# Moving three elementwise steps of the feed-forward part from VectorE to ScalarE in a Mamba-plus-ternary-FFN kernel

## The chip, the cores and the metric

The kernel runs as one program on all 8 cores of one Trainium2 chip. Each core works on its own 2048 tokens; there is no traffic between the cores apart from their common memory. The metric is the device time in microseconds (us) of the slowest core, and the profile is of that core (core 7 here). The engines are PE (TensorE), DVE (VectorE), ACT (ScalarE), POOL (GpSimd) and SP (SyncE), each with its own instruction queue that it works through in order.

## The reference

For 16384 tokens of 1024 numbers, the output is `x + mamba(layernorm(x)) + ffn(layernorm(x))`. Only the feed-forward part is touched by the change:

```python
def _act_quant(x):
    scale = 127.0 / clip(max(abs(x), axis=-1), 1e-05)
    return clip(round(x * scale), -128.0, 127.0) / scale
def _weight_quant(w):
    scale = 1.0 / clip(mean(abs(w)), 1e-05)
    return clip(round(w * scale), -1.0, 1.0) / scale
bitlinear = lambda x, w: einsum('bsi,oi->bso', _act_quant(x), _weight_quant(w))
ffn = lambda x: bitlinear(silu(bitlinear(x, w_gate)) * bitlinear(x, w_up), w_down)
```

The hidden width is 4096. Quantised activations are integers up to 127 and quantised weights are -1, 0 or 1; both are held in bf16, and the scales are multiplied in when a result leaves PSUM.

## The kernel before, in words

A small recording layer (`P.op`) takes each instruction with the names of what it reads and writes, puts it at the end of its engine's queue, and adds the waits on semaphores that those names ask for. The order in each queue is therefore the order in which the Python code calls `P.op`; generators that yield one instruction at a time are interleaved by hand. A buffer that is written again waits for its last reader.

The program has four stages on each core: layer norm and the casting of weights; the Mamba part with its scans (most of the time); F1, the gate and up projections with silu; and F2, the down projection and the final sum. A barrier over all queues stands between the stages. The change is in F1 and F2.

**F1** runs over 8 column blocks f of 512 columns. For each f, `f1_mm(f)` runs over 16 token tiles mt of 128 tokens. A tile is 8 matmuls into a gate bank, 8 into an up bank, and then four steps: gsb (L918, ACT, silu of the gate bank times a per-token scale), usb (L921, DVE, the up bank times a per-token scale), gu_bf (L924, DVE, the product of the two) and gmparts (L928, DVE, its largest magnitude). There are three gate banks (psB, psG2, psG3) and three up banks (psC, psU2, psU3), used in turn, and two buffers each of gsb and usb. So the first up matmul of tile mt+3 waits for usb of tile mt, and gsb of tile mt waits for gu_bf of tile mt-2.

Beside the tiles of block f, a second stream `_sec(f)` does two other jobs. It quantises the gate and up weights for block f+1: a load from HBM on SP into one of two buffers wqf, then L891 and L895 on DVE, sixteen times. And in blocks 0 to 5 it quantises the down weights: a load into the single buffer wqf3, then L957 and L960 on DVE into the single buffer wdstg, and a store on POOL (L965) to the HBM tensor s_wdq. `_zipf` takes two steps of the tiles, then one of the second stream, so the second stream lies beside tiles 0 to 7 of a block, and tiles 8 to 15 have the engines to themselves. This document calls these the first and the second half of a block.

**F2** runs over 8 groups g of two token tiles. `f2_a(g)` requantises the hidden activations in four pieces per tile: tqg (L1041, DVE, scale and add the rounding bias 384.5), a mask (L1047, DVE), minus 384 (L1050, DVE, back into gu_bf); then 8 transposes per piece on PE (L1058) into the one bank psT, and ACT copies them out to guqT (L1065). `f2_b(g)` does the down matmuls (L1089) for both tiles, psB for the first and psC for the second, over two halves of 512 output columns. It loads 1 MB of s_wdq for every 16 matmuls into one of two buffers wdqt, ends each half with two scalings dnsb (L1100, DVE), and each group with four adds (L1108, L1112, DVE) and a store. `f2_a(g+1)` is interleaved with `f2_b(g)`, two steps to three, so one tile's requantising lies beside each half; `f2_a(0)` stands alone at the start of F2. There are two buffers tqg; the mask works in place.

Of the kernel before, what the change touches and what calls it, by code (L numbers as in the profile page):

```python
# [11 lines left out]
AF = mybir.ActivationFunctionType  # L12
ALU = mybir.AluOpType
# [12 lines left out]
RBIAS = 384.5  # L26
# [116 lines left out]
def build_program(TOK):  # L143
# [29 lines left out]
    P = Prog(nc)  # L173
# [4 lines left out]
    def salloc(stack, name, shape, dt):  # L178
        return stack.enter_context(nc.sbuf_tensor(name, shape, dt))
# [8 lines left out]
    combou = salloc(pstack, "combou", [128, NT], F32)  # L188
    combod = salloc(pstack, "combod", [128, NT], F32)
    gmparts = salloc(pstack, "gmparts", [128, NT * 8], F32)  # L190
    sgu = salloc(pstack, "sgu", [128, NT], F32)
    invsgu = salloc(pstack, "invsgu", [128, NT], F32)
    ones1 = salloc(pstack, "ones1", [128, 1], F32)
    csts = salloc(pstack, "csts", [128, 3], F32)
# [607 lines left out]
    for sc in range(NSC):  # L802
# [7 lines left out]
        else:  # L810
# [12 lines left out]
                            for t2 in range(32)],  # L823
         writes=["psA"], wr_override=["psA"])
    P.op("scalar", lambda s: s.activation(acc[0:1, 0:96], psA[0:1, 0:96], AF.Copy,
                                          bias=0.0, scale=1.0),
# [31 lines left out]
    usb = [salloc(fstk, "usb%d" % i, [128, 512], BF16) for i in range(2)]  # L858
# [42 lines left out]
    def f1_mm(f):  # L901
        fb = f % 2
        for mt in range(NT):
            gb = mt % 2
            psg, psgt = psGpool[mt % 3]
            psu, psut = psUpool[mt % 3]
            for (wtag, ps_, pst_) in (("wgq", psg, psgt), ("wuq", psu, psut)):
                wq_ = wgq[fb] if wtag == "wgq" else wuq[fb]
                for k2 in range(8):
                    yield lambda wq_=wq_, k2=k2, mt=mt, ps_=ps_, pst_=pst_, wtag=wtag, fb=fb: P.op(  # L910
                        "tensor", lambda t: t.matmul(  # L911
                            ps_[:, 0:512],
                            xqfm[:, k2 * TOK + mt * 128:k2 * TOK + (mt + 1) * 128],
                            wq_[:, k2 * 512:(k2 + 1) * 512], start=(k2 == 0), stop=(k2 == 7)),
                        reads=["xqfm:%d" % k2, "%s:%d:%d" % (wtag, fb, k2)],
                        writes=([pst_] if k2 == 0 else ()),
                        wr_override=([pst_] if k2 == 7 else ()))
            yield lambda gb=gb, mt=mt, psg=psg, psgt=psgt: P.op("scalar", lambda s: s.activation(  # L918
                gsb[gb][:], psg[:, 0:512], AF.Silu, bias=0.0, scale=combog[:, mt:mt + 1]),
                reads=[psgt, "cg:%d" % mt], writes=["gsb:%d" % gb])  # L920
            yield lambda gb=gb, mt=mt, psu=psu, psut=psut: P.op("vector", lambda v: v.tensor_single_scalar(  # L921
                usb[gb][:], psu[:, 0:512], combou[:, mt:mt + 1], ALU.mult),
                reads=[psut, "cu:%d" % mt], writes=["usb:%d" % gb])
            yield lambda gb=gb, mt=mt, f=f: P.op("vector", lambda v: v.tensor_mul(  # L924
                gu_bf[:, mt * INNER + f * 512:mt * INNER + (f + 1) * 512],
                gsb[gb][:], usb[gb][:]),
                reads=["gsb:%d" % gb, "usb:%d" % gb], writes=["gu:%d:%d" % (mt, f)])
            yield lambda gb=gb, mt=mt, f=f: P.op("vector", lambda v: v.reduce_max(  # L928
                gmparts[:, mt * 8 + f:mt * 8 + f + 1],
                gu_bf[:, mt * INNER + f * 512:mt * INNER + (f + 1) * 512],  # L930
                axis=AXX, apply_absolute_value=True),
                reads=["gu:%d:%d" % (mt, f)], writes=["gmp:%d:%d" % (mt, f)])
# [62 lines left out]
    for f in range(8):  # L995
        _zipf(iter(f1_mm(f)), _sec(f), 2, 1)
# [33 lines left out]
    dnsb = [salloc(f2stk, "dnsb%d" % i, [128, DM], F32) for i in range(2)]  # L1030
# [4 lines left out]
    def f2_a(g):  # L1035
        gb = g % 2
        mts = (2 * g, 2 * g + 1)
        for j, mt in enumerate(mts):
            for hh in range(4):
                hb = hh % 2  # L1040
                yield lambda mt=mt, hh=hh, hb=hb: P.op("vector", lambda v: v.tensor_scalar(  # L1041
                    tqg[hb][:], gu_bf[:, mt * INNER + hh * 1024:mt * INNER + (hh + 1) * 1024],
                    sgu[:, mt:mt + 1], RBIAS, ALU.mult, ALU.add),
                    reads=["gu:%d:%d" % (mt, f2) for f2 in range(hh * 2, hh * 2 + 2)]
                          + ["sgu:%d" % mt],
                    writes=["tqg:%d" % hb])
                yield lambda hb=hb: P.op("vector", lambda v: v.tensor_single_scalar(  # L1047
                    tmg[hb][:].bitcast(I32), tqg[hb][:].bitcast(I32), RMASK, ALU.bitwise_and),
                    reads=["tqg:%d" % hb], writes=["tqg:%d" % hb])
                yield lambda mt=mt, hh=hh, hb=hb: P.op("vector", lambda v: v.tensor_single_scalar(  # L1050
                    gu_bf[:, mt * INNER + hh * 1024:mt * INNER + (hh + 1) * 1024],
                    tmg[hb][:], -384.0, ALU.add),
                    reads=["tqg:%d" % hb] + ["gu:%d:%d" % (mt, f2) for f2 in range(hh * 2, hh * 2 + 2)],
                    writes=["guqq:%d:%d" % (mt, hh)])
            for gb8 in range(4):
                for kb in range(8):
                    kk = gb8 * 8 + kb
                    yield lambda mt=mt, kk=kk, kb=kb: P.op("tensor", lambda t: t.matmul(  # L1058
                        psT[:, kb * 128:(kb + 1) * 128],
                        gu_bf[:, mt * INNER + kk * 128:mt * INNER + (kk + 1) * 128],  # L1060
                        eye[:], is_transpose=True, start=(kb == 0), stop=(kb == 7)),
                        reads=["guqq:%d:%d" % (mt, kk // 8), "eye"],
                        writes=(["psT"] if kb == 0 else ()),
                        wr_override=(["psT"] if kb == 7 else ()))
                yield lambda j=j, gb8=gb8, gb=gb: P.op("scalar", lambda s: s.activation(  # L1065
                    guqT[gb][j][:, gb8 * 1024:(gb8 + 1) * 1024], psT[:, 0:1024], AF.Copy,
                    bias=0.0, scale=1.0),
                    reads=["psT"], writes=["guqT:%d:%d:%d" % (gb, j, gb8)])

    def f2_b(g):  # L1070
        gb = g % 2
        mts = (2 * g, 2 * g + 1)
        for f2 in range(2):
            for kc in range(4):
                wb3 = kc % 2
                yield lambda kc=kc, f2=f2, wb3=wb3: P.op("sync", lambda e: e.dma_start(
                    wdqt[wb3][:].rearrange("part (k c) -> part k c", k=8),
                    s_wdq.ap()[kc * 1024:(kc + 1) * 1024,
                               f2 * 512:(f2 + 1) * 512].rearrange(
                        "(k part) c -> part k c", k=8)),  # L1080
                    reads=["swdq:%d:%d" % (kc * 8 + k3, f2) for k3 in range(8)],
                    writes=["wdqt:%d" % wb3], dma=True)
                for k3 in range(8):
                    kb = kc * 8 + k3
                    for j, mt in enumerate(mts):
                        ps_ = psB if j == 0 else psC
                        pst_ = "psB" if j == 0 else "psC"
                        yield lambda j=j, kb=kb, k3=k3, wb3=wb3, ps_=ps_, pst_=pst_, gb=gb: P.op(
                            "tensor", lambda t: t.matmul(  # L1089
                                ps_[:, 0:512], guqT[gb][j][:, kb * 128:(kb + 1) * 128],  # L1090
                                wdqt[wb3][:, k3 * 512:(k3 + 1) * 512],
                                start=(kb == 0), stop=(kb == 31)),
                            reads=["guqT:%d:%d:%d" % (gb, j, kb // 8), "wdqt:%d" % wb3],
                            writes=([pst_] if kb == 0 else ()),
                            wr_override=([pst_] if kb == 31 else ()))
            for j, mt in enumerate(mts):
                ps_ = psB if j == 0 else psC
                pst_ = "psB" if j == 0 else "psC"
                yield lambda j=j, mt=mt, f2=f2, ps_=ps_, pst_=pst_: P.op(
                    "vector", lambda v: v.tensor_single_scalar(  # L1100
                        dnsb[j][:, f2 * 512:(f2 + 1) * 512], ps_[:, 0:512],
                        combod[:, mt:mt + 1], ALU.mult),
                    reads=[pst_, "cd:%d" % mt], writes=["dn:%d:%d" % (j, f2)])
        for j, mt in enumerate(mts):
            yield lambda j=j, mt=mt: P.op("sync", lambda e: e.dma_start(
# [14 lines left out]
    for fn in f2_a(0):  # L1120
        fn()
    for g in range(NT // 2):
        nxt = iter(f2_a(g + 1)) if g + 1 < NT // 2 else iter(())
        _zipf(iter(f2_b(g)), nxt, 3, 2)
# [82 lines left out]
```

How the kernel before makes its waits and increments, by code:

```python
                def body(eng, lst=lst, q=q):  # L119
                    sat = {}
                    last_inc = {}
                    for o in lst:
                        wl = {}
                        for d in o.waits:
                            if d.cum > wl.get(d.skey, 0):
                                wl[d.skey] = d.cum
                        for k in sorted(wl, key=lambda t: (t[0], t[1])):
                            v = wl[k]
                            if v > sat.get(k, 0):
                                eng.wait_ge(sems[k], v)
                                sat[k] = v
                        inst = o.fn(eng) if o.fn is not None else None
                        if o.inc:
                            k = o.skey
                            amt = o.cum - last_inc.get(k, 0)
                            inst.then_inc(sems[k], amt)
                            last_inc[k] = o.cum
```

## Time and profile before

| what | value |
|---|---|
| median of 2 timed runs | 5410.28 us (5409.01 to 5411.56) |
| the profiled execution's own time | 5414.21 us |
| its span (core 7, first to last instruction) | 5412.6 us; 5371.2 to 5412.6 us over the cores |
| DVE busy over the span | 4078.4 us (75%) |
| ACT busy over the span | 1691.7 us (31%) |
| PE busy over the span | 1658.3 us (31%) |
| F1's blocks, by the trace | 4335 to 4963 us of the span |
| F2, by the trace | 4984 to 5413 us of the span |

The busy shares are averages over stages with different limits, so what the change is worth has to be read inside F1 and F2. A row of the timeline gives an instruction's start, its length, its engine, its line, and in square brackets how long its engine sat idle before it and what ended the idle time. The chain of waits follows the last instruction of a stretch back to what released it, step by step.

### The profile page before, as it was taken

What the parts mean: (1) busy time and instruction counts of PE and PEld (TensorE: products, weight loads), DVE (VectorE), ACT (ScalarE), POOL (GpSimd) and SP (SyncE); (2) the same over time, 40 slices, a digit from 0 to 9 for tenths busy, and PEclk for the clock granted to TensorE, in tenths of its full rate; (3) what the DMA queues carried; (4) which work ended last, traced back from release to release, by engine and by line L of the source; (5) the groups of instructions that cost most, each with busy time, mean ns of one, the idle gap of its engine ahead of it and who ended that gap; (6) DMA issues with size and microseconds to landing.
All of it is one profiled execution on the core that took longest, in us unless ns stands there. A gap on an engine that the chain in (4) does not pass through costs nothing.

```text
span 5412.6 us, 45661 instructions; the slowest of 8 cores (5371.2 to 5412.6 us)
## 1 busy us (share of the span) xinstructions
PE 1658.3 (31%) x7308; PEld 830.6 (15%) x7308; DVE 4078.4 (75%) x10959; ACT 1691.7 (31%) x3882; POOL 212.0 (4%) x380
## 2 busy tenths in 40 slices
PE   0013410321151032114113201411100277777776
PEld 0002200210020021002002100200000023233332
DVE  2333888888888888888888888888888677766443
ACT  1234435343433444343333432433222111111111
POOL 1450000000000000000000000000000000000000
PEclk9997655655565565557556555755555589898999
DMA  5512203210330141033002100300100232320566
GB/s 184 179 51 80 63 0 98 77 32 0 102 104 0 51 125 32 0 105 110 0 0 78 35 0 16 97 0 0 47 0 0 92 118 89 112 87 22 188 214 204
DMA packets 316917, 378.33 MB, mean 70 GB/s; under 512 B 19346, under 2 KB 257042, under 8 KB 314516
## 3 DMA queue, kind: packets, MB, share of 16 engines
q1 hardware_dynamic: 296596, 316.68, 19.2%
q0 software_dynamic: 18304, 46.16, 2.3%
q10 hardware_dynamic: 1728, 12.58, 0.7%
q14 instruction: 223, 1.83, 0.1%
q8 instruction: 66, 1.08, 0.1%
HBM read 329.22 MB, written 46.14 MB: 69 GB/s over the span
## 4 chain that ended last, share of the span: by engine, by line
DVE 43%; issue 16%; DMA 14%; PE 14%; ACT 9%; DVEq 1%; POOL 1%; SPq 0%; ACTq 0%; POOLq 0%
DVE hbuf L658 17%; DVE dbub L651 8%; DVE ypb L672 5%; ACT dAb L642 4%; DVE yA L675 3%; DMA wdqt<-s_wdq 3%; PE psBC L621 3%; PE psBC L628 2%; DMA s_wdq<-wdstg 2%; DMA wch<-s_winT 1%; DMA wo_buf<-s_woutT 1%; PE psU L911 1%; DMA wqf<-wuT 1%; PE psB L1089 1%; DMA wqf<-wgT 1%
## 5 line engine op out<-in xcount | busy, mean ns | idle before, releaser
L658 DVE TENSOR_TENSOR_SCAN hbuf<-dAb,dbub 128x256 bf16<-128x256 bf16 x2048 | 1399.7, 683 | 164.5 <-ACT dAb L642 164.5
L675 DVE TENSOR_TENSOR yA<-yA,ypb 128x256 f32<-128x256 f32 x1920 | 816.5, 425 | 204.0 <-DVE ypb L672 6.0
L642 ACT ACTIVATE dAb<-delta_t,alneg 128x256 bf16<-128x256 bf16 x2048 | 905.6, 500 | 48.1 <-DVE hbuf L658 46.4
L621 PE MATMUL psBC<-shstB,ones 1*128 1x256 f32 x256 | 148.2, 679 | 2075.7 <-DVE shstB L618 2075.5
L632 ACT ACTIVATE Bsb<-psBC 128x256 bf16<-128x256 f32 x128 | 49.2, 384 | 1947.4 <-PE psBC L628 1892.8
L651 DVE TENSOR_TENSOR dbub<-du_t,Bsb 128x256 bf16<-128x256 bf16 x2048 | 581.2, 284 | 6.0 <-ACT Bsb L632 2.4
L672 DVE TENSOR_TENSOR ypb<-hbuf,Csb 128x256 bf16<-128x256 bf16 x1920 | 511.3, 266 | 0.0
L621 PEld LDWEIGHTS psBC<-shstB,ones 1*128 1x128 f32 x256 | 62.0, 299 | 2129.9 <-issue 2129.9
L491 PE MATMUL psI<-xnsc,wch 128*128 128x256 bf16 x2048 | 324.9, 327 | 141.0 <-DMA wch<-s_winT 129.4
L491 PEld LDWEIGHTS psI<-xnsc,wch 128*128 128x128 bf16 x2048 | 227.9, 116 | 243.3 <-issue 185.0
L725 PE MATMUL psOut<-wo_buf,gated 128*128 128x512 bf16 x256 | 119.2, 466 | 445.0 <-DVE gated L697 384.7
L1089 PE MATMUL psB<-wdqt,guqT 128*128 128x512 bf16 x512 | 207.6, 405 | 63.2 <-DMA wdqt<-s_wdq 54.0
L1089 PE MATMUL psC<-wdqt,guqT 128*128 128x512 bf16 x512 | 207.2, 405 | 2.1 <-DVE dnsb L1100 2.1
L911 PE MATMUL psU<-wuq,xqfm 128*128 128x512 bf16 x640 | 177.1, 427 | 99.1 <-DVE usb L921 99.0
L1100 DVE TENSOR_SCALAR dnsb<-psB,combod 128x512 f32<-128x512 f32 x16 | 12.0, 750 | 212.8 <-PE psB L1089 212.8
L1065 ACT ACTIVATE guqT<-psTf 128x1024 bf16<-128x1024 bf16 x64 | 65.5, 1024 | 334.1 <-PE psTf L1058 307.9
L918 ACT ACTIVATE gsb<-psG,combog 128x512 bf16<-128x512 f32 x80 | 55.0, 687 | 343.8 <-DVE gu_bf L924 136.6
L911 PE MATMUL psG<-wgq,xqfm 128*128 128x512 bf16 x640 | 160.1, 395 | 0.0
L742 POOL DMA_DIRECT2D s_mm<-mmo x16 | 8.5, 532 | 3864.5 <-DVE mmo L737 3228.9
L628 PE MATMUL psBC<-shstC,ones 1*128 1x256 f32 x256 | 131.9, 615 | 0.0
L582 PE MATMUL psB<-dltbf,wdtT_bf 64*128 64x256 bf16 x128 | 48.0, 375 | 251.9 <-ACT xpb L586 231.7
L780 ACT ACTIVATE wab<-wab 128x1024 f32<-128x1024 f32 x96 | 101.3, 1055 | 68.1 <-DMA wab<-wdT 25.1
(148 smaller groups left out, 3261.8 us busy)
## 6 DMA issues: line engine op xcount, KB each, us to landing
wch<-s_winT SPq DMA_DIRECT2D x128, 512.0 KB, 4.3
wdqt<-s_wdq SPq DMA_DIRECT2D x64, 1024.0 KB, 6.3
wo_buf<-s_woutT SPq DMA_DIRECT2D x64, 512.0 KB, 4.5
wab<-wgT SPq DMA_DIRECT2D x32, 512.0 KB, 4.2
wab<-wuT SPq DMA_DIRECT2D x32, 512.0 KB, 4.3
wab<-wdT SPq DMA_DIRECT2D x32, 512.0 KB, 4.3
wqf<-wgT SPq DMA_DIRECT2D x64, 256.0 KB, 3.4
wqf<-wuT SPq DMA_DIRECT2D x64, 256.0 KB, 3.2
```

The lines of the kernel that those rows point to most:

```text
L491: "tensor", lambda t: t.matmul(psI[mp][:, 0:CH], wch[wb][:, k2 * 256 + m * 128:k2 * 256 + (m + 1) * 128], xnsc[p][:, k2 * CH:(k2 + 1) * CH ...
L621: P.op("tensor", lambda t, bk=bk: t.matmul(psBC[bk][:, 0:CH], ones2[64:65, 0:128], shstB[64:65, :], start=True, stop=True), reads=["shB", ...
L628: P.op("tensor", lambda t, bk=bk: t.matmul(psBC[bk][:, CH:2 * CH], ones2[64:65, 0:128], shstC[64:65, :], start=True, stop=True), reads=["s ...
L642: P.op("scalar", lambda s, q=q, n=n, b=b: s.activation(dAb[b][:], delta_t[p][:, q * CH:(q + 1) * CH], AF.Exp, bias=0.0, scale=alneg[:, q * ...
L651: P.op("vector", lambda v, q=q, b3=b3, e2=e2: v.tensor_mul(dbub[b3][:], du_t[p][:, q * CH:(q + 1) * CH], Bsb[e2][:]), reads=["du:%d:%d" % ...
L658: P.op("vector", lambda v, b=b, b3=b3: v.tensor_tensor_scan(hbuf[b3][:], dAb[b][:], dbub[b3][:], 0.0, ALU.mult, ALU.add), reads=["dA:%d" % ...
L672: P.op("vector", lambda v, q=q, b=b, b3=b3, e2=e2: v.tensor_mul(ypb[b][:], hbuf[b3][:], Csb[e2][:]), reads=["h:%d" % b3, "Csb:%d" % e2], w ...
L675: P.op("vector", lambda v, q=q, b=b: v.tensor_add(yA[:, q * CH:(q + 1) * CH], yA[:, q * CH:(q + 1) * CH], ypb[b][:]), reads=["yA:%d" % q, ...
L725: "tensor", lambda t: t.matmul(ps_[:, 0:512], gated[p][:, kq * CH + mtok * 128:kq * CH + (mtok + 1) * 128], wo_buf[wb2][:, j * 512:(j + 1) ...
L780: yield lambda wi=wi, t=t, b=b: P.op("scalar", lambda sx: sx.activation(wab[b][:], wab[b][:], AF.Abs, bias=0.0, scale=1.0, accum_out=acc[: ...
L911: "tensor", lambda t: t.matmul(ps_[:, 0:512], xqfm[:, k2 * TOK + mt * 128:k2 * TOK + (mt + 1) * 128], wq_[:, k2 * 512:(k2 + 1) * 512], sta ...
L1089: "tensor", lambda t: t.matmul(ps_[:, 0:512], guqT[gb][j][:, kb * 128:(kb + 1) * 128], wdqt[wb3][:, k3 * 512:(k3 + 1) * 512], start=(kb == ...
```

## The change

Three DVE steps become ACT activations that compute the same: usb (L921, 128 of 128x512 from PSUM), tqg (L1041, 64 of 128x1024), and dnsb (L1100, 32 of 128x512 from PSUM). Buffers, banks, matmuls, loads and the order in which the code calls `P.op` stay as they are, so the steps keep their place among the others but stand in another queue.

```diff
             yield lambda gb=gb, mt=mt, psg=psg, psgt=psgt: P.op("scalar", lambda s: s.activation(
                 gsb[gb][:], psg[:, 0:512], AF.Silu, bias=0.0, scale=combog[:, mt:mt + 1]),
                 reads=[psgt, "cg:%d" % mt], writes=["gsb:%d" % gb])
-            yield lambda gb=gb, mt=mt, psu=psu, psut=psut: P.op("vector", lambda v: v.tensor_single_scalar(
-                usb[gb][:], psu[:, 0:512], combou[:, mt:mt + 1], ALU.mult),
+            yield lambda gb=gb, mt=mt, psu=psu, psut=psut: P.op("scalar", lambda s: s.activation(
+                usb[gb][:], psu[:, 0:512], AF.Copy, bias=0.0, scale=combou[:, mt:mt + 1]),
                 reads=[psut, "cu:%d" % mt], writes=["usb:%d" % gb])
...
-                yield lambda mt=mt, hh=hh, hb=hb: P.op("vector", lambda v: v.tensor_scalar(
+                yield lambda mt=mt, hh=hh, hb=hb: P.op("scalar", lambda s: s.activation(
                     tqg[hb][:], gu_bf[:, mt * INNER + hh * 1024:mt * INNER + (hh + 1) * 1024],
-                    sgu[:, mt:mt + 1], RBIAS, ALU.mult, ALU.add),
+                    AF.Identity, bias=csts[:, 2:3], scale=sgu[:, mt:mt + 1]),
                     reads=["gu:%d:%d" % (mt, f2) for f2 in range(hh * 2, hh * 2 + 2)]
-                          + ["sgu:%d" % mt],
+                          + ["sgu:%d" % mt, "cst2"],
                     writes=["tqg:%d" % hb])
...
                 yield lambda j=j, mt=mt, f2=f2, ps_=ps_, pst_=pst_: P.op(
-                    "vector", lambda v: v.tensor_single_scalar(
-                        dnsb[j][:, f2 * 512:(f2 + 1) * 512], ps_[:, 0:512],
-                        combod[:, mt:mt + 1], ALU.mult),
+                    "scalar", lambda s: s.activation(
+                        dnsb[j][:, f2 * 512:(f2 + 1) * 512], ps_[:, 0:512], AF.Copy,
+                        bias=0.0, scale=combod[:, mt:mt + 1]),
                     reads=[pst_, "cd:%d" % mt], writes=["dn:%d:%d" % (j, f2)])
```

In the queue of DVE, in the first half of block f = 1 of F1, a piece of the difference around usb of tile 3 (wqf0 and wqf1 are the two buffers for the gate and up weights, wqf3 the one for the down weights):

```order
 L891 TENSOR_SCALAR wts<-wqf1,swbc 128x512
 L895 SCALAR_TENSOR_TENSOR wgq0<-wqf1,swbc,wts 128x512
-L921 TENSOR_SCALAR usb1<-psC,combou 128x512
 L957 TENSOR_SCALAR wts<-wqf3,swbc 128x512
 L960 SCALAR_TENSOR_TENSOR wdstg<-wqf3,swbc,wts 128x512
```

Only usb leaves the queue; what stood behind it moves up.

In the queue of ACT, at the start of F1's first block, a piece of the difference:

```order
 L918 ACTIVATE gsb0<-psB,combog 128x512
+L921 ACTIVATE usb0<-psC,combou 128x512
 L918 ACTIVATE gsb1<-psG2,combog 128x512
+L921 ACTIVATE usb1<-psU2,combou 128x512
 L918 ACTIVATE gsb0<-psG3,combog 128x512
+L921 ACTIVATE usb0<-psU3,combou 128x512
```

ACT now empties both banks of a tile, gate first, in the order of the tiles.

In the queue of ACT at the start of F2, first the rows before (the first number of guqT is its group's parity, the second its tile in the group; x4 stands for four in a row):

```order
L1065 ACTIVATE guqT0_0<-psTf 128x1024 x4
L1065 ACTIVATE guqT0_1<-psTf 128x1024 x4
L1065 ACTIVATE guqT1_0<-psTf 128x1024 x4
```

and the same place with the change, from the second tile of group 0 on:

```order
L1065 ACTIVATE guqT0_0<-psTf 128x1024 x4
L1041 ACTIVATE tqg0<-gu_bf,csts,sgu 128x1024
L1041 ACTIVATE tqg1<-gu_bf,csts,sgu 128x1024
L1041 ACTIVATE tqg0<-gu_bf,csts,sgu 128x1024
L1041 ACTIVATE tqg1<-gu_bf,csts,sgu 128x1024
L1065 ACTIVATE guqT0_1<-psTf 128x1024 x4
```

The four tqg of a tile now stand behind the four copies of the tile before it, and ahead of their own tile's copies. Later, where a half of `f2_b` ends, the piece reads:

```order
L1065 ACTIVATE guqT1_0<-psTf 128x1024 x3
L1100 ACTIVATE dnsb0<-psB,combod 128x512
L1100 ACTIVATE dnsb1<-psC,combod 128x512
L1065 ACTIVATE guqT1_0<-psTf 128x1024
L1041 ACTIVATE tqg0<-gu_bf,csts,sgu 128x1024
```

There the two dnsb and the last guqT of a tile stand ahead of the next tile's first tqg.

## Rows read from the trace of the kernel before

**Rows 1.** Block 1, block 7, F2: length; busy PE, PEld, DVE, ACT, POOL; PEclk; DMA.
```profile
4417.09:4498.99 81.90, 62.70 (x256) 26.16 (x255) 59.95 (x101) 10.64 (x17) 5.40 (x10) 0.90 0.30 100
...
4908.90:4963.50 54.60, 53.08 (x246) 23.87 (x244) 29.14 (x49) 10.70 (x16) 0.00 (x0) 1.00 0.00 1
4983.69:5412.60 428.91, 295.14 (x1536) 134.69 (x1536) 191.57 (x256) 65.55 (x64) 11.48 (x16) 0.90 0.62 197
```

**Rows 2.** What PE waited for ahead of line L911 (us, times).
```profile
  DVE usb L921: 137.6, 42
```

**Rows 3.** Chain of waits of block f = 1: start us, us, what.
```profile
4446.37 3.28 DMA s_wdq<-wdstg
...
4475.23 0.76 DVE usb L921
4476.12 3.50 PE psU L911 x8
4479.63 1.73 PE psG L911 x8
...
4495.17 1.74 PE psC L911 x8
```

**Rows 4.** Timeline of DVE: first and last of 14 long waits for weight loads.
```profile
4354.37 0.49 DVE L891 TENSOR_SCALAR wts<-wqf,swbc 128x512 f32<-128x512 f32 x1 [2.57 <-DMA wqf<-wgT]
...
4812.88 0.48 DVE L891 TENSOR_SCALAR wts<-wqf,swbc 128x512 f32<-128x512 f32 x1 [2.72 <-DMA wqf<-wuT]
...
4814.13 0.74 DVE L921 TENSOR_SCALAR usb<-psU,combou 128x512 bf16<-128x512 f32 x1
4814.80 0.48 DVE L957 TENSOR_SCALAR wts<-wqf,swbc 128x512 f32<-128x512 f32 x1
```

**Rows 5.** Line L924: durations in ns (min/median/max), and who waited for it.
```profile
L924 DVE TENSOR_TENSOR gu_bf<-gsb,usb x128: 415/426/427, 4341.3 to 4962.9; 128x512 bf16<-128x512 bf16 x128
...
  ACT gsb L918: 203.1, 40
```

**Rows 6.** Groups of instructions: busy us, mean ns of one | idle before.
```profile
L366 ACT ACTIVATE tq<-xn,csts,sxs 128x1024 f32<-128x1024 f32 x16 | 19.8, 1240 | 51.7 <-DVE sxs L363 51.7
...
L918 ACT ACTIVATE gsb<-psG,combog 128x512 bf16<-128x512 f32 x80 | 55.0, 687 | 343.8 <-DVE gu_bf L924 136.6 <-PE psG L911 122.8 <-PE psU L911 40.0
L921 DVE TENSOR_SCALAR usb<-psU,combou 128x512 bf16<-128x512 f32 x80 | 59.7, 746 | 33.3 <-PE psU L911 33.0
L1041 DVE TENSOR_SCALAR tqg<-gu_bf,sgu 128x1024 f32<-128x1024 bf16 x64 | 47.8, 747 | 0.1
L1047 DVE TENSOR_SCALAR tqg<-tqg 128x1024 int32<-128x1024 int32 x64 | 44.4, 694 | 7.4 <-DVE tqg L1041 0.9
L1065 ACT ACTIVATE guqT<-psTf 128x1024 bf16<-128x1024 bf16 x64 | 65.5, 1024 | 334.1 <-PE psTf L1058 307.9 <-DMA bob<-b_out_bc 26.3
L918 ACT ACT_TABLE_LOAD x1 | 1.3, 1283 | 30.5 <-PE psB L911 30.5
```

**Rows 7.** Timeline of F2's start, DVE, ACT and PE.
```profile
4983.69 0.75 DVE L1041 TENSOR_SCALAR tqg<-gu_bf,sgu 128x1024 f32<-128x1024 bf16 x1
...
4989.84 1.02 ACT L1065 ACTIVATE guqT<-psTf 128x1024 bf16<-128x1024 bf16 x1 [1.47 <-PE psTf L1058]
...
5004.65 0.63 PE L1089 MATMUL psB<-wdqt,guqT 128*128 128x512 bf16 x1
```

**Rows 8.** Timeline of F2 where a group and where a half ends.
```profile
5106.62 0.75 DVE L1100 TENSOR_SCALAR dnsb<-psB,combod 128x512 f32<-128x512 f32 x1 [16.59 <-PE psB L1089]
...
5115.35 0.37 PE L1058 MATMUL psTf<-eye,gu_bf 128*128 128x128 bf16 x2 [2.23 <-DVE gu_bf L1050]
...
5135.01 0.75 DVE L1100 TENSOR_SCALAR dnsb<-psB,combod 128x512 f32<-128x512 f32 x1 [13.02 <-PE psB L1089]
...
5143.44 0.28 PE L1058 MATMUL psTf<-eye,gu_bf 128*128 128x128 bf16 x2
```

**Rows 9.** Waits in F2 alone: us in total, times, longest us.
```profile
PE psTf L1058 <- DVE gu_bf L1050: 31.1, 7, 24.2
```

## The prediction

> **What bounds the kernel now.** I began with the busy time per stretch, since the change touches only F1 and F2. Block 7 of F1 has no second stream: it takes 54.6 us, PE is busy for 53.1 of them at a granted clock of 1.00, and that is what a block costs when only PE limits it. Block 1, with the second stream, takes 81.9 us, and DVE, busy 60 of them, is not full either [rows 1]. So in blocks 0 to 6 something other than PE's speed or DVE's speed costs over 20 us a block. What PE waits for ahead of its F1 matmuls names it: 137.6 us in 42 waits, all for usb on DVE [rows 2]. The chain of waits of block 1 then says when this matters. Through the first half of the block it is a relay of transfers and weight quantising on DVE: a load of wqf releases L891, the store of wdstg (3.28 us) releases the next L960. From 4475.23 on it is another chain: usb of tile 7, then eleven groups of 8 matmuls, psU of tile 10 first, up to psC of tile 15 [rows 3]. In the first half a wait of PE costs nothing, because the relay is longer. At the end of that half PE stands still behind usb of tile 7, three tiles ahead of DVE, and the rest is run at PE's pace, 1.73 us a group. So two questions decide F1: how much of the relay consists of usb, and how far ahead PE may be when it ends.
>
> In F2 DVE is busy 192 of 429 us, ACT 66, PE 295 [rows 1]. PE waits 31.1 us for gu_bf there, of which 24.2 us is the one wait at the start of F2 and 6.9 us the other six [rows 9].
>
> **The change part by part: F1.** The 128 usb leave DVE at 746 ns each and come to ACT. The trace has no copy of this shape with a scale per token. The nearest is silu, same bank, same output, same kind of scale, 687 ns; the copy of L1065 takes 1024 ns for 1024 columns, which bounds it above [rows 6]. I take 687. ACT loaded its table once for L918, and L1065 behind it, a copy, has no load of its own [rows 6], so I count no table loads.
>
> *How far PE may run ahead.* Before, usb of tile 7 stands in DVE's queue right ahead of gu_bf of tile 7, and psU of tile 10 needs it. With the change usb is on ACT behind gsb, and both wait only for their buffers, that is, for gu_bf two tiles earlier. That gsb has this limit already is seen: it waited 40 times, 203.1 us, for gu_bf [rows 5]. So when gu_bf of tile 7 ends, usb of tile 8 is long done and psU of tile 11 with it. The next group in want is psG of tile 12, which waits for gsb of tile 9, and that for gu_bf of tile 7. PE's lead is two tiles longer, at the price of one ACT step. Let E be the end of usb of tile 7 before. From there to the end of tile 15 it is 0.14 us (4475.23 plus 0.75, to 4476.12) and 11 groups of 1.73, 19.2 us at full clock [rows 3]. After, DVE has no usb to do, so gu_bf ends at E - 0.75 + 0.43 [rows 5]; then 0.14, gsb 0.69 and 0.14 again put psG of tile 12 at E + 0.65; 8 groups of 1.73 remain, ending at E + 14.5. The gain is 4.7 us a block. Blocks 0 to 5 have this form, and block 6 too, with a shorter second stream: 7 x 4.7 = 33 us. From below, 0 if PE's lead is held by something else; from above two whole tiles, 4 x 1.73 = 6.9 us a block, 48 us. The first group in these rows took 3.50 us instead of 1.73, at half clock after the wait, and some blocks show it and some not; I leave it equal on both sides, and it is worth up to 1.8 us a block either way.
>
> *What usb takes of the relay.* It takes part only where nothing but DVE follows it before the next transfer. There are 14 waits of over 2.4 us for a weight load in blocks 0 to 5, and right behind each stand L895, usb, and the pair L957 and L960, whose store starts the next link [rows 4]. Without usb the pair comes 0.66 us sooner (4814.13 to 4814.80). In two of the 14 that usb is tile 7's, counted already; 12 x 0.66 = 8 us. The other usb of the first halves lie ahead of a wait for a load that was issued earlier or for the store, so these waits grow by what DVE saves. I count them as 0; if half of the remaining 28 counted it would be 9 us more. Block 6 may add 1. In the second halves and block 7 usb is followed by gu_bf on the same chain, and 687 plus 0.14 in place of 746 is nothing. F1 in all: 33 + 8 + 1 = 42 us less.
>
> **F2.** The 64 tqg go from 747 ns to ACT, where L366 does the same function with the same two operands per partition in 1240 ns; that is with f32 input, and 1024 ns bounds it from below [rows 6]. I take 1240. They come to an engine that also copies out the transposes, in order.
>
> *The start.* Before, tqg of the second tile runs on DVE while the first tile is transposed; from the first tqg to the first L1089 it is 20.96 us, and the copies follow each other every 2.49 us, 1.47 of waiting and 1.02 of work [rows 7]. After, with the mask and the subtraction at some 0.7 us each on DVE [rows 6] and two buffers, the fourth tqg ends at 5.6 us, and the first copy stands behind it: copies at 5.6, 8.1, 10.6 and 13.05, the last ending at 14.1. Only then come the four tqg of the second tile, the last ending at 19.65, and four more copies: 19.65, 22.1, 24.6. Right behind the seventh, PE does the eighth set of transposes (1 us at 26.0) and begins L1089 at about 26.8. That is 5.8 us more.
>
> *Ends of a group.* From dnsb at 5106.62 DVE does two dnsb and four adds before the next tqg, and PE waits 2.23 us for gu_bf at 5115.35 [rows 8]. After, tqg and dnsb run on ACT beside the adds: the first gu_bf ends at 7.25 us after dnsb instead of 8.6. That is worth up to 1.35 us, of six waits that together are 6.9 us [rows 9]: 6 us less at most.
>
> *Ends of a half inside a group.* Here the next tqg stands behind two dnsb and one copy on ACT: it starts 2.5 us after dnsb instead of 1.3, and gu_bf ends at 5.3 instead of 3.7. PE wants it at 8.4 (5135.01 to 5143.44) [rows 8]. The load in between covers that; without the load PE would come at about 6, still later. 0 us. The 32 dnsb, 746 to 687, give 1 us at most.
>
> F2 in all: 5.8 - 6 = 0 us, from -8 (if the gains stand and the start costs less) to +15 (if each of the 14 later tiles also loses 0.7).
>
> The Trainium skill (ScalarE: Activation LUTs, section Rules for kernel authors) says to put adds and multiplies on VectorE and not on ScalarE, with VectorE up to three times as fast in bf16. The trace agrees for tqg, 747 against 1240 ns, and not for the reads from PSUM, where ScalarE's 687 stands against 746 [rows 6]. By the rule alone the change should lose; that is the third rival.
>
> **The sum.** 5414.2 (the profiled execution's own time) - 42 + 0 = 5372 us. That execution was 3.9 us above the median of the runs shown, so I predict 5369.
>
> **The rivals.** *First, the lead is not gained.* If the two buffers of gsb and not usb hold PE back, only the 9 us of the relay and block 6 remain: 5405 for the profiled execution, about 5400 for the median. For it: the 203.1 us that gsb waits for gu_bf [rows 5]. Against: all 42 of PE's waits that name an engine's release of a bank name usb, none gsb [rows 2].
>
> *Second, DVE's whole saving is on the path.* Then all 48 usb of the first halves count 0.66 us, 32 us in place of 8, and the lead 48 in place of 33: 42 + 24 + 15 = 81 us, about 5330. For it: DVE is the busiest engine of the stretch [rows 1]. Against: the chain goes through transfers, such as the store's 3.28 us, which do not shorten [rows 3].
>
> *Third, ACT's queue becomes F2's bound, and the kernel is slower.* Four tqg stand ahead of the first copy of their tile, 4 x 1.24 = 5.0 us; if PE's single transpose bank waits for that at each of the 14 later tiles, F2 costs 70 + 5.8 = 76 us more, and the time is 5410 - 42 + 76 = 5444. It decides from 36 / 14 = 2.6 us a tile on. For it: the start of F2, where just this costs 2.9 us a tile. Against: PE comes to a tile's transposes 8.4 us after dnsb [rows 8], when most of the tqg are done.
>
> **How the numbers follow.** The forecast holds with 0.72, the first rival 0.12, the second 0.06, the third 0.08, other things 0.02. The forecast's own range is 5345 to 5400 (the lead from 2.5 to 6 us a block, the relay from 4 to 15, F2 from -8 to +15). The range given, 5345 to 5406, takes in the first rival and leaves out the second, most of the third and the rest, 0.16. About 2%, 108 us, is what a measurement of this kernel can tell from no change; the forecast is 0.8% faster, and only stacked versions of the second or third rival go past 2%: faster 0.02, within 0.96, slower 0.02.
>
> **What would show it.** Right: blocks 0 to 5 some 6 us shorter each and block 7 as before; PE's eleven last groups become eight; the 14 long waits for weight loads stay, the shorter ones grow; the first L1089 comes 26 to 27 us after the first tqg. Wrong: blocks 0 to 5 shorter by less than 3 us or more than 10, a table load on ACT beside L921 or L1041, or waits of PE for the copies L1065 that grow by tens of us in F2.

## The result and the profile after

The changed kernel takes 5370.33 us (median of 9 runs, 5364.97 to 5381.7); the kernel before, beside it, 5410.28 us (8 runs, 5404.19 to 5415.57). The ratio is 0.9928, with a 95% interval from 0.9917 to 0.9938: 40 us less, where 5369 was forecast.

The profile is of core 1, with a span of 5356.5 us; that execution took 5358.33 us, 12 us less than its median. F1 starts some 5 to 12 us earlier in it although nothing ahead of F1 was changed, so the two profiled executions lie further apart (56 us) than the kernels do, and only F1 and F2 are compared below.

Busy time in block 1, in block 7 and in F2, after; the columns are those of [rows 1], PE, PEld, DVE, ACT, POOL, PEclk, DMA share and GB/s:

```profile
4406.77:4482.47 75.70, 60.91 (x258) 25.92 (x257) 48.50 (x85) 20.80 (x33) 5.40 (x10) 0.91 0.34 108
4865.01:4920.27 55.26, 53.15 (x247) 23.87 (x244) 17.79 (x33) 21.78 (x32) 0.00 (x0) 1.00 0.00 1
4939.50:5356.50 417.00, 285.79 (x1536) 131.64 (x1536) 124.19 (x161) 160.64 (x160) 10.67 (x16) 0.91 0.64 203
```

Block 1 is 6 us shorter than in [rows 1]. Block 7, which only PE limits, is as long as it was: its row in [rows 1] stops at 4963.50, 0.7 us before its last gmparts ended, and counted to that end it took 55.3 us before and after. DVE lost 11 us of work in block 1, and the block took 6 us less. The split of all blocks, from the timeline of DVE (a block ends with the last gmparts, its first half with gu_bf of tile 7; block 0 begins with the first L891 of the second stream, and the row of F2 with the end of block 7):

| us | before, core 1 | before, core 7 | after, core 1 | after, core 7 |
|---|---|---|---|---|
| the 8 blocks of F1 | 626.6 | 629.0 | 590.1 | 588.8 |
| first half, mean of blocks 0 to 5 | 62.2 | 61.8 | 60.5 | 60.0 |
| rest of the block, mean of blocks 0 to 5 | 21.6 | 22.2 | 18.2 | 18.5 |
| block 6 | 68.4 | 69.7 | 62.9 | 62.7 |
| F2, to the last work of DVE | 431.3 | 439.8 | 427.7 | 421.3 |

F1 loses 36.5 us on one core and 40 on the other, two thirds of it behind the last tile that the second stream lies beside (tile 7; tile 4 in block 6, whose second stream is shorter). F2 differs by 6 to 9 us between two cores of one execution, and with the code of after it took from 420.6 to 441.0 us in the runs below, so nothing can be read from its length alone.

What PE waited for ahead of L911, after; and under the line of gu_bf, who waited for it:

```profile
  ACT gsb L918: 111.3, 35
...
  ACT gsb L918: 280.7, 47
```

usb is gone from the list; in [rows 2] it stood there with 137.6 us. PE now waits for gsb, and gsb for gu_bf: 280.7 us (core 1) where [rows 5] had 203.1 (core 7). The limit is the pair of gsb buffers, two tiles further on; two of the runs below change their number.

The chain of waits of block 1, after (start, us, what):

```profile
4427.27 0.76 DVE wdstg L960
4428.10 0.33 SPq L953
4428.53 3.67 DMA wqf<-wgT
4432.37 0.50 DVE wts L891
...
4459.37 3.38 DMA s_wdq<-wdstg
...
4462.91 0.76 DVE wdstg L960
...
4465.03 0.43 DVE gu_bf L924
4465.54 0.70 ACT gsb L918
...
4466.48 1.89 PE psB L911 x8
4468.37 1.73 PE psC L911 x8
...
4478.73 1.73 PE psC L911 x8
```

The first half is still the relay of transfers and quantising. Its last link is now gu_bf of tile 7, which releases gsb of tile 9, and that the gate bank for tile 12. From 4466.48 to the end of 4478.73's group there are eight groups of 8 matmuls; [rows 3] had eleven. The first four rows show something that the prediction passed over: the link from L960 to the weight load goes through SP's queue at L953, the load into wqf3. Two of the runs below follow that up.

Waits of DVE for the second stream's transfers, after (lines L891, L957 and L960):

```profile
  DMA wqf<-wuT: 44.4, 28
  DMA wqf<-wgT: 44.1, 23
...
  DMA wqf<-wdT: 23.4, 30
...
  DMA s_wdq<-wdstg: 18.3, 29
```

Before, on core 7, these four were 34.6, 37.6, 8.0 and 19.1 us. They grew by 31 us together (by 27.5 on core 1 as well as on core 7, each compared with itself), and the 48 usb that left the first halves took 48 times 0.66, 32 us. Most of the time that DVE won there was spent waiting for the same transfers. The long waits for a weight load are 14 again, of 2.7 to 3.0 us; the first and the last, in the timeline of DVE:

```profile
4349.31 0.49 DVE L891 TENSOR_SCALAR wts<-wqf,swbc 128x512 f32<-128x512 f32 x1 [2.80 <-DMA wqf<-wgT]
...
4779.91 0.49 DVE L891 TENSOR_SCALAR wts<-wqf,swbc 128x512 f32<-128x512 f32 x1 [2.78 <-DMA wqf<-wuT]
```

Groups of instructions, after (busy us, mean ns of one | idle before):

```profile
L1041 ACT ACTIVATE tqg<-gu_bf,csts,sgu 128x1024 f32<-128x1024 bf16 x64 | 77.5, 1238 | 47.6 <-DVE gu_bf L1050 26.8 <-DVE combod L1016 20.8
L921 ACT ACTIVATE usb<-psU,combou 128x512 bf16<-128x512 f32 x80 | 55.0, 687 | 38.9 <-PE psU L911 37.7 <-PE psG L911 1.3
L1100 ACT ACTIVATE dnsb<-psB,combod 128x512 f32<-128x512 f32 x16 | 11.0, 687 | 70.1 <-PE psB L1089 70.1
L918 ACT ACT_TABLE_LOAD x1 | 1.3, 1283 | 29.2 <-PE psB L911 29.2
```

F2's start, timeline of ACT and PE, after:

```profile
4939.79 2.37 ACT L1041 ACTIVATE tqg<-gu_bf,csts,sgu 128x1024 f32<-128x1024 bf16 x2 [20.85 <-DVE combod L1016]
...
4953.77 2.36 ACT L1041 ACTIVATE tqg<-gu_bf,csts,sgu 128x1024 f32<-128x1024 bf16 x2
...
4966.38 0.63 PE L1089 MATMUL psB<-wdqt,guqT 128*128 128x512 bf16 x1
```

Three of the waits in F2 alone, after (us in total, times, longest):

```profile
PE psB L1089 <- DMA wdqt<-s_wdq: 54.0, 33, 5.3
PE psTf L1058 <- ACT guqT L1065: 46.1, 46, 2.8
PE psTf L1058 <- DVE gu_bf L1050: 5.2, 3, 4.0
```

The first down matmul comes 26.6 us after the first tqg, 20.96 before [rows 7]: the second tile's tqg, at 4953.77, had to wait for the four copies of the first. Of the 5.2 us of waits for gu_bf, 4.0 belong to this start, so the waits at the ends of the groups fell from 6.9 us [rows 9] to 1.2. These waits differ between cores of one execution: on core 1 of the kernel before they are 12.8 us, on core 7 of the kernel after 2.6.

### The profile page after: what moved, and what is told of

Its sections match the earlier page's. It is cut to its first block, busy times and chain, and to the rows that moved or that the text cites. A ratio compares the mean times of both kernels' runs of the same rounds, so it can differ in the third digit from the quotient of the medians.

```text
span 5356.5 us, 45957 instructions; the slowest of 8 cores (5329.5 to 5356.5 us)
## 1 busy us (share of the span) xinstructions
PE 1621.8 (30%) x7308; PEld 820.0 (15%) x7308; DVE 3921.9 (73%) x10735; ACT 1865.9 (35%) x4106; POOL 211.5 (4%) x380
## 4 chain that ended last, share of the span: by engine, by line
DVE 43%; issue 16%; DMA 15%; PE 14%; ACT 10%; DVEq 1%; POOL 1%; SPq 0%; ACTq 0%; POOLq 0%
DVE hbuf L658 17%; DVE dbub L651 8%; DVE ypb L672 5%; ACT dAb L642 4%; DMA wdqt<-s_wdq 3%; DVE yA L675 3%; PE psBC L621 3%; PE psBC L628 2%; DMA wo_buf<-s_woutT 2%; DMA s_wdq<-wdstg 2%; DMA wch<-s_winT 1%; DMA wqf<-wgT 1%; DMA wqf<-wuT 1%; PE psB L1089 1%; DMA wcf<-w_inT 1%
## 5 line engine op out<-in xcount | busy, mean ns | idle before, releaser
L632 ACT ACTIVATE Bsb<-psBC 128x256 bf16<-128x256 f32 x128 | 49.2, 384 | 1934.9 <-PE psBC L628 1767.3
L911 PE MATMUL psG<-wgq,xqfm 128*128 128x512 bf16 x640 | 168.3, 410 | 70.4 <-ACT gsb L918 70.1
L911 PE MATMUL psU<-wuq,xqfm 128*128 128x512 bf16 x640 | 158.3, 392 | 0.0
L1047 DVE TENSOR_SCALAR tqg<-tqg 128x1024 int32<-128x1024 int32 x64 | 44.2, 691 | 142.8 <-ACT tqg L1041 142.3
L918 ACT ACTIVATE gsb<-psG,combog 128x512 bf16<-128x512 f32 x80 | 55.1, 689 | 222.0 <-DVE gu_bf L924 179.5
L891 DVE TENSOR_SCALAR wts<-wqf,swbc 128x512 f32<-128x512 f32 x128 | 62.0, 485 | 94.4 <-DMA wqf<-wuT 44.4
```

The source lines that it names most:

```text
L911: "tensor", lambda t: t.matmul(ps_[:, 0:512], xqfm[:, k2 * TOK + mt * 128:k2 * TOK + (mt + 1) * 128], wq_[:, k2 * 512:(k2 + 1) * 512], sta ...
```

## The experiments

**Which of the moves gives the time.** One kernel moves usb alone: from the changed kernel, tqg and dnsb go back to DVE.

```diff
-                yield lambda mt=mt, hh=hh, hb=hb: P.op("scalar", lambda s: s.activation(
+                yield lambda mt=mt, hh=hh, hb=hb: P.op("vector", lambda v: v.tensor_scalar(
...
-                    "scalar", lambda s: s.activation(
+                    "vector", lambda v: v.tensor_single_scalar(
```

> Only usb (L921) moves to ACT; tqg and dnsb stay on DVE. Theory (PE's lead in F1 grows by two tiles, and usb leaves the relay only behind the 14 long waits for weight loads; F2 balances out): 5410 - 42 = 5368 us, ratio 0.992, blocks 0 to 6 of F1 shorter by 5 to 7 us each, F2 as before. Rival (the gain came from F2, where the two profiles differ by 4 us on core 1 and 18 us on core 7): 5395 to 5406 us.

Measured 5370.44 us (5 runs), ratio 0.9921, 0.9907 to 0.9935: all that the whole change gives. The other kernel moves the two steps of F2 alone, and usb goes back to DVE.

```diff
-            yield lambda gb=gb, mt=mt, psu=psu, psut=psut: P.op("scalar", lambda s: s.activation(
+            yield lambda gb=gb, mt=mt, psu=psu, psut=psut: P.op("vector", lambda v: v.tensor_single_scalar(
```

> Only tqg and dnsb move to ACT; usb stays on DVE. Theory: the start of F2 loses 5.8 us (first tqg to first down matmul 26.7 instead of 21.0 us), the group ends give back up to 6 us: 5410 us, ratio 1.000, between 0.9985 and 1.0015. Rival one (F2 itself became faster, as the profiles of core 7 suggest): 5392 to 5402 us. Rival two (ACT's queue costs F2 time that F1's gain hid): 5420 us or more.

Measured 5410.8 us (11 runs), ratio 0.9997, 0.9988 to 1.0005: nothing, between 6.5 us less and 2.7 us more. F2's first down matmul comes 26.6 us after the first tqg here too, so the 5.6 us lost at the start are won back elsewhere in F2. The shorter waits at the ends of its groups are of that size; no run shows what they are worth alone.

**Is it PE's lead.** If the gain is the number of tiles that PE may be ahead when gu_bf of tile 7 ends, the number of gsb buffers must set it. With one buffer, gsb of a tile waits for gu_bf of the tile before it:

```diff
-    gsb = [salloc(fstk, "gsb%d" % i, [128, 512], BF16) for i in range(2)]
-    usb = [salloc(fstk, "usb%d" % i, [128, 512], BF16) for i in range(2)]
+    gsb = [salloc(fstk, "gsb%d" % i, [128, 512], BF16) for i in range(1)]
+    usb = [salloc(fstk, "usb%d" % i, [128, 512], BF16) for i in range(1)]
...
-            gb = mt % 2
+            gb = mt % 1
```

> The changed kernel with one buffer each of gsb and usb instead of two. Theory: gsb of a tile waits for gu_bf of the tile right before, so PE's lead at the end of a first half shrinks by one tile (ten groups of 1.73 us remain after gu_bf of tile 7 instead of eight), 3.45 us for each of 7 blocks: 24 us slower than the changed kernel, about 5394 us. Rival (the gain is DVE's freed time, not the lead): 5370 us, as with two buffers.

Measured 5397.32 us, ratio 0.9972, 0.996 to 0.9984. The chain of waits of its block 1, behind gu_bf of tile 7:

```profile
4480.38 0.43 DVE gu_bf L924
...
4480.89 0.69 ACT gsb L918
...
4481.83 1.89 PE psG L911 x8
4483.72 1.73 PE psU L911 x8
...
4497.53 1.73 PE psC L911 x8
```

Ten groups instead of eight; the rest of a block takes 21.7 us on average (blocks 0 to 5 of core 7) instead of 18.5 on the same core of the kernel after, two groups of 1.73 more. The first halves stay at 59.9. Two thirds of the gain are gone although usb is still on ACT: a place off DVE is worth a third of it by itself, some 13 to 15 us.

The other way, usb goes straight into its place in gu_bf, where no pair of buffers limits it any more, and this frees the room for four gsb:

```diff
-    gsb = [salloc(fstk, "gsb%d" % i, [128, 512], BF16) for i in range(2)]
-    usb = [salloc(fstk, "usb%d" % i, [128, 512], BF16) for i in range(2)]
+    gsb = [salloc(fstk, "gsb%d" % i, [128, 512], BF16) for i in range(4)]
...
-                usb[gb][:], psu[:, 0:512], AF.Copy, bias=0.0, scale=combou[:, mt:mt + 1]),
-                reads=[psut, "cu:%d" % mt], writes=["usb:%d" % gb])
+                gu_bf[:, mt * INNER + f * 512:mt * INNER + (f + 1) * 512],
+                psu[:, 0:512], AF.Copy, bias=0.0, scale=combou[:, mt:mt + 1]),
+                reads=[psut, "cu:%d" % mt], writes=["ub:%d:%d" % (mt, f)])
```

> The changed kernel with usb written straight to its place in gu_bf (multiplied there in place) and four buffers of gsb in the same memory. Theory: gsb of a tile waits for gu_bf four tiles back, PE's lead grows by two more tiles, four groups remain after gu_bf of tile 7; the time from gu_bf of tile 7 to the end of a block falls from 17 to 20 us to about 10, 7 us for each of 7 blocks: 5370 - 48 = 5322 us. Rival (the lead no longer decides, DVE's relay does): 5365 to 5370 us.

Measured 5324.59 us, ratio 0.9843, 0.9826 to 0.986. In its block 1 gu_bf of tile 7 ends at 4456.46, and the chain of waits around it is (L911 is L910 and L918 is L917 in this kernel):

```profile
4449.82 0.43 DVE gu_bf L924
...
4450.34 0.70 ACT gsb L917
...
4451.28 3.57 PE psG L910 x8
...
4458.13 1.24 PE psG L910 x5
4459.37 1.73 PE psU L910 x8
4461.10 1.73 PE psB L910 x8
4462.83 1.73 PE psC L910 x8
```

Behind that time four groups are left, those of tiles 14 and 15 (the first of them is broken in two pieces, of which the second stands here). PE is hardly held by gu_bf of tile 7 any more: in this block its last wait is the one ahead of 4451.28, for gsb of tile 10, which gu_bf of tile 6 had released at 4450.25. The rest of a block takes 11.7 us on average. Ten, eight and four groups go with 21.7, 18.2 to 18.5 and 11.7 us: 1.6 to 1.75 us a group.

**Would the buffers do it without the move.** The same two edits with usb, tqg and dnsb on DVE, as in the kernel before; the hunk of usb, against the changed kernel:

```diff
-            yield lambda gb=gb, mt=mt, psu=psu, psut=psut: P.op("scalar", lambda s: s.activation(
-                usb[gb][:], psu[:, 0:512], AF.Copy, bias=0.0, scale=combou[:, mt:mt + 1]),
+            yield lambda gb=gb, mt=mt, f=f, psu=psu, psut=psut: P.op("vector", lambda v: v.tensor_single_scalar(
+                gu_bf[:, mt * INNER + f * 512:mt * INNER + (f + 1) * 512],
+                psu[:, 0:512], combou[:, mt:mt + 1], ALU.mult),
```

> The kernel before (usb on DVE) with usb written straight to its place in gu_bf and four buffers of gsb. Theory: usb stays in DVE's queue right ahead of gu_bf, so the up matmuls of tile mt+3 still wait for DVE at tile mt, however many buffers there are: 5410 us, ratio 1.000 (0.998 to 1.002). Rival (it was the number of buffers that held PE, and the engine of usb is a side matter): 5360 to 5380 us.

Measured 5409.25 us (10 runs), ratio 1.0, 0.999 to 1.001: nothing. What PE waited for ahead of the gate and up matmuls (the upward scaling now goes by the name of its place, gu_bf, and has the line L920):

```profile
  DVE gu_bf L920: 121.4, 40
```

It is the row of [rows 2] again. While the step that empties the up bank stands in DVE's queue behind tile 7's quantising, two more gsb change nothing: the release of the up bank was the limit before, and the buffers became it after.

**The relay.** The chain above shows the gate and up loads held in SP's queue behind the load for wqf3 (L953), which waits for L960 to release its one buffer. SP works in order, so a load whose buffer is free stands behind one whose buffer is not. Here each gate and up load is issued one round earlier, ahead of that one (_wld holds the same load, k counts the sixteen of a block):

```diff
-                yield lambda wsrc=wsrc, k2=k2, f=f, b=b: P.op("sync", lambda e: e.dma_start(
-                    wqf[b][:], wsrc.ap()[k2 * 128:(k2 + 1) * 128, f * 512:(f + 1) * 512]),
-                    writes=["wqf:%d" % b], dma=True)
+                kk = col * 8 + k2
+                yield lambda kk=kk: [_wld(f, k) for k in
+                                     ((0, 1) if kk == 0 else (kk + 1,)) if k < 16]
```

> The changed kernel, with each gate or up weight load called one round earlier, so that in SP's queue it no longer stands behind the down weight load that waits for L960. No instruction is added and DVE's order is the same. Theory (a relay of transfers bounds the first halves of blocks 0 to 5): the 14 or so long waits for weight loads go, the store and load of the down weights remain as the bound, some 5.0 us for each of 10.7 pairs a block, 53 us instead of 59: about 5 us for each of 6 blocks, 5340 us. Rival (DVE's own work bounds the first halves): 5370 us, with the waits only moved.

Measured 5312.9 us, ratio 0.9821, 0.9806 to 0.9836: 57 us less than the change alone, where some 30 were expected. DVE's waits for the second stream (L891, L957 and L960 are L898, L964 and L967 in this kernel):

```profile
  DMA wqf<-wgT: 18.9, 12
  DMA wqf<-wuT: 13.1, 16
...
  DMA wqf<-wdT: 34.4, 45
...
  DMA s_wdq<-wdstg: 5.1, 6
```

The four sum to 71.5 us; after the change alone they summed to 130.2. The difference, 59 us, is about the gain. None of the 14 long waits for a gate or up load is left: in blocks 0 to 5 the longest is 0.8 us. The first halves take 50.8 us instead of 60.5, and the rests of the blocks are as before (17.9). The expectation was too small: in the timelines the steps L957 of block 1 followed each other after 4.3 to 5.0 and 7.1 to 7.5 us in turn, two in 12.0; here L964 comes every 4.5 to 5.4 us, two in 9.6. That is also the link that remains: load (3.1 us), L964, L967 and the next load. In the first half of block 1 (4398.1 to 4447.3) DVE's waits over 0.3 us, seven and together 5.1 us, are all for this load. DVE is busy for 39.1 of these 49.2 us and PE for 42.8, so at most some 10 us a block are left to win from the transfers, an estimate from DVE's busy time.

Both together, with the edits of the runs with four gsb and with earlier loads:

```diff
+    gsb = [salloc(fstk, "gsb%d" % i, [128, 512], BF16) for i in range(4)]
...
+                yield lambda kk=kk: [_wld(f, k) for k in
+                                     ((0, 1) if kk == 0 else (kk + 1,)) if k < 16]
```

> Four buffers of gsb with usb in place, and the early weight loads, together. Theory: the two gains are in different halves of a block and add up: 5325 - 31 = 5294 us. Rival (with shorter first halves PE can't use the longer lead): 5310 us or more.

Measured 5267.07 us, ratio 0.9739, 0.9724 to 0.9753. Below the change alone the two gains were 45.7 and 57.4 us; together they are 103.3. They add, because one shortens the first half of a block and the other the rest: the first halves take 50.8 us, as with the earlier loads alone, and the rests 11.9, as with four gsb alone (11.7). That the sum is met to 0.1 us is chance, for each of these times is known to some 8 us. What was expected, 5294, is 27 us more, as the gain of the earlier loads had been put at 30. Block 1, in the columns of [rows 1]:

```profile
4402.48:4462.68 60.20, 55.65 (x251) 24.54 (x249) 48.05 (x85) 20.40 (x32) 5.52 (x10) 0.97 0.44 136
```

PE is busy for 55.7 of 60.2 us: the block is now close to block 7, which PE alone limits.

And the same with the first group's tqg back on DVE:

```diff
+                if g > 0:
                     yield lambda mt=mt, hh=hh, hb=hb: P.op("scalar", lambda s: s.activation(
...
+                else:
+                    yield lambda mt=mt, hh=hh, hb=hb: P.op("vector", lambda v: v.tensor_scalar(
```

> As the kernel before it in this list (four buffers of gsb, early weight loads), with the tqg of group 0 alone on DVE again. Theory: from the first tqg to the first down matmul 21.0 us instead of 26.6, 5.6 us less: 5288 us, and 0.999 of the time without it. Rival (the start of F2 is hidden by the first loads of s_wdq): the same time as without it.

Measured 5260.83 us, ratio 0.9724, 0.9709 to 0.9739, the lowest time here. F2's start in the timeline (L1056 is tqg of group 0 and L1104 the down matmul here):

```profile
4837.62 0.75 DVE L1056 TENSOR_SCALAR tqg<-gu_bf,sgu 128x1024 f32<-128x1024 bf16 x1
...
4858.63 0.63 PE L1104 MATMUL psB<-wdqt,guqT 128*128 128x512 bf16 x1
```

From the first tqg to the first down matmul it is 21.0 us again, against 26.8 in the kernel just above (4844.60 to 4871.43). The medians differ by 6.2 us and agree with these 5.8, but the intervals of the two ratios overlap, so the gain in time rests on the timeline.

## Why the prediction was right

- **The durations.** usb was taken at 687 ns and measured at 687; tqg at 1240, measured 1238; dnsb at 687, measured 687 and 680. No table load was added: L918 has its one, and L921, L1041 and L1100 have none.
- **PE's lead.** The step was right in its form: eleven groups became eight, released by gu_bf of tile 7 through gsb of tile 9. The 4.7 us a block were counted from the end of usb of tile 7; from gu_bf of tile 7, which itself was to come 0.75 us sooner, they are 3.95. Measured are 3.4 us on core 1 and 3.7 on core 7, so the term was right in form and a little too large. Block 6 has the same form with tile 4 in place of tile 7: behind its second stream 17 groups became 14 (the chains of waits from 4875.70 before and from 4838.57 after), and the block lost 5.5 and 7.0 us, 5.7 by the prediction.
- **The relay.** The first halves were to lose 0.75 us, the move of gu_bf of tile 7, and 8 / 6 = 1.3, together 2.05; they lost 1.7 and 1.8. All 14 long waits for weight loads stayed, and the shorter ones grew by nearly what DVE saved, as costed. This is where the rival with DVE's whole saving on the path fell.
- **F1 in all.** 42 us were forecast; 36.5 and 40 stand in the two profiled executions, and 41 in the times of the kernel with usb alone (5411.87 - 5370.44).
- **F2.** The start was worked out to come at 26.8 us and came at 26.6. From the first dnsb at the end of a group to the first gu_bf after it was 8.60 us and is 7.28 at five of the six ends, 7.63 at one (7.25 by the prediction); inside a group it was 3.67 and is 5.3 to 6.9 (5.3 by the prediction), and PE never waited for that gu_bf. PE's waits at the ends of the groups fell by 5.7 us, of the 6 that were the most they could give. PE's waits for the copies at its transposes went from 37.9 to 46.1 us, and 5.5 of these 8.2 us fall in F2's start. That is far from the 76 us of the rival in which ACT's queue bounds F2. The sum, nothing, is what the kernel with F2's moves alone shows.
- **The rival without a gain in lead** had named the right limit, the two gsb buffers, but at the wrong place: they hold PE only two tiles later. The runs with one and with four buffers show that they do.

The Trainium skill (ScalarE: Activation LUTs, section Rules for kernel authors) sends adds and multiplies to VectorE. For tqg the runs agree at the start of F2, where nothing else lies beside it: putting that group's tqg back took 5.8 us from the timeline. In the rest of F2 they show no loss. For usb, which reads PSUM, they do not: the move to ScalarE gave all of the 40 us.

What was right partly by luck: that 5369 lies 1.3 us from the measured time. The lead came out a little smaller than its 4.7 us a block, and the nothing of F2 is the difference of two sums, of which the gain at the ends of the groups was read from one core (6.9 us of waits, 12.8 on another core of the same execution). The profiled execution of after was 12 us below its median, and that profile alone would have put the gain at 56 us. Two slips in the working changed little: the usb left over beside the relay are 30 and not 28 (48 less 12 and less the six of tile 7), and 5372 less 3.9 is 5368. The 2% that the prediction calls the least that can be told from no change is too much: the interval here is 6 us either way, and it tells 40 us from nothing.

## What to carry to other kernels

When an engine's work is moved off a busy queue, its busy time is not the gain: follow which bank or buffer it releases, count how many steps the consumer may then run ahead, and look for the next thing that limits it. Moving the step and adding buffers belong together: here more buffers alone gave nothing, the move alone 40 us, both 87. Where a wait on a transfer stands on the chain, look at which instruction its issue stood behind; reordering the loads on top of the move gave 57 us, more than the move. What the reordering gives without the move was not run.

## What the runs showed that was not expected

PE's granted clock was not the same behind each wait. In the kernel after, PE stood idle for 0.98 us ahead of 4466.48 in block 1, and for 8.05 us ahead of 4548.54 in block 2. The first group behind each wait, and what follows the second, in the columns of [rows 1]:

```profile
4466.48:4468.37 1.89, 1.89 (x9) 0.88 (x10) 1.68 (x4) 1.89 (x4) 0.00 (x0) 1.00 0.51 189
...
4548.54:4552.10 3.56, 3.56 (x9) 1.28 (x10) 3.15 (x8) 2.61 (x5) 0.00 (x0) 0.50 0.47 161
4552.11:4566.00 13.89, 13.89 (x66) 6.23 (x64) 4.33 (x8) 5.50 (x8) 0.00 (x0) 0.99 0.01 2
```

After the long wait the first group of eight ran at half clock, 1.2 GHz, and took 3.57 us instead of 1.89; only the next ones came back to 2.4 GHz. In block 1 such a group, 3.57 us long behind a wait of 5.55, had come one tile earlier, at 4460.20, while the relay still ran, and cost nothing. This is the 1.8 us a block that the prediction left equal on both sides. In the table's terms, the rest of block 1 took 17.1 us and that of block 2 took 19.4. The length of the wait alone does not decide: in the kernel before, the group at 4476.12 [rows 3] ran at half clock behind a wait of 2.77 us, and the one at 4805.47 at full clock behind 3.00. Why the long wait falls ahead of the last groups in one block and earlier in another was not followed further.

Two gains of 46 and 57 us in the same eight blocks added up in full, and the second, a change in the order in which SP issues the loads on top of the move, gave twice what was expected of it.
